# Moving work on TensorE in four attention stages of a transformer kernel, with repeated matmuls ahead of one of them

## What is computed

```python
x = x + _L1_xattn_ref(_layernorm(x), ctx, ctx, mask, ...)      # 16 heads, softmax over 77 keys
...
scores = jnp.einsum('bqhd,bkhd->bhqk', q, k) / np.sqrt(DK)     # _L1_ffn_ref: self attention,
attn = jax.nn.softmax(scores, axis=-1)                         # 16 heads of 16, 1024 x 1024 per head
o = jnp.einsum('bhqk,bkhd->bqhd', attn, v)
...
def sparse_norm(scores, nbias):                                # _L2_xattn_ref: no softmax
    t = jax.nn.relu(scores + nbias[0])
    t = t * t
    return t / (t.sum(-1, keepdims=True) + IEPS)
...
x = x + _L3_xattn_ref(_layernorm(x), ctx, ...)                 # 16 heads, softmax over 77 keys
```

## Time and profile before

| | |
|---|---|
| median of 3 runs | 2685.7 us (2677.44 to 2688.1) |
| the profiled execution | 2695.88 us |
| its span, first to last instruction | 2694.1 us |
| granted TensorE clock, mean | 0.887 |
| TensorE busy | 2201.1 us (82%) |
| VectorE busy | 1298.8 us (48%) |
| ScalarE busy | 1087.3 us (40%) |
| GpSimd busy | 651.7 us (24%) |

### The profile page before, as it was taken

The page is one execution under the profiler, slowest core; times in us unless marked ns, Lnnn a source line. Parts: engine busy times, 40 slices in busy tenths (PEclk is TensorE's granted clock), DMA queues, the critical chain, the costliest instruction groups (busy, mean ns, idle before and its releaser), DMA issues. The chain is left out here.

```text
span 2694.1 us, 36343 instructions
## 1 busy us (share of the span) xinstructions
PE 2201.1 (82%) x12198; PEld 1304.1 (48%) x12199; DVE 1298.8 (48%) x2560; ACT 1087.3 (40%) x2189; POOL 651.7 (24%) x569
## 2 busy tenths in 40 slices
PE   5899999953948766999998399994976999767786
PEld 2333333242933431333333299994345999633454
DVE  5655555165154557578871600004452350164785
ACT  3434444420314511566666244442532444325111
POOL 1238888911520050000000022220001222110011
PEclk9899999985977885699999699997887999978898
DMA  2000000022610053223420665652036666400000
GB/s 64 5 1 13 13 10 13 25 67 91 203 59 1 20 148 40 32 32 45 51 33 1 190 214 195 199 191 89 1 118 233 198 201 203 138 13 1 0 1 32
DMA packets 141630, 214.34 MB, mean 80 GB/s; under 512 B 39600, under 2 KB 97644, under 8 KB 141500
## 3 DMA queue, kind: packets, MB, share of 16 engines
q1 hardware_dynamic: 131228, 186.10, 25.3%
q0 software_dynamic: 9696, 26.49, 2.6%
q10 hardware_dynamic: 576, 0.07, 0.0%
HBM read 182.00 MB, written 30.15 MB: 79 GB/s over the span
## 5 line engine op out<-in xcount | busy, mean ns | idle before, releaser
L1840 DVE TENSOR_REDUCE heads_part_max<-heads_shared_ps 128x2 f32<-128x1024 f32 x256 | 300.1, 1220 | 93.5 <-PE heads_shared_ps L1757 93.5
L1824 ACT ACTIVATE heads_probs<-heads_score_ps 128x512 f32<-128x512 f32 x512 | 266.4, 603 | 194.4 <-PE heads_score_ps L1779 194.4
L2873 PE MATMUL experts_up_ps<-experts_rowT,experts_w 128*128 128x128 f32 x2864 | 342.9, 279 | 0.0
L2873 PEld LDWEIGHTS experts_up_ps<-experts_rowT,experts_w 128*128 128x128 f32 x2864 | 334.9, 195 | 0.2
L3033 DVE TENSOR_TENSOR experts_y<-experts_down_ps,experts_b_now 128x256 f32<-128x256 f32 x78 | 33.1, 425 | 499.5 <-PE experts_down_ps L2883 499.3
L1354 POOL TENSOR_TENSOR core_xT<-core_xT,heads_probs 128x1024 f32<-128x1024 f32 (+1 forms) x112 | 264.4, 2360 | 24.0 <-ACT heads_probs L1527 10.5
L2941 ACT ACTIVATE experts_hT<-experts_up_ps,experts_b_now 128x128 f32<-128x128 f32 x624 | 222.8, 367 | 49.0 <-PE experts_up_ps L2873 11.8
L1566 DVE TENSOR_REDUCE heads_part_max<-heads_shared_ps 128x1 f32<-128x512 f32 x256 | 164.5, 686 | 146.7 <-PE heads_shared_ps L1396 146.5
L1779 PE MATMUL heads_score_ps<-heads_q,heads_k 66*128 66x512 f32 x512 | 199.4, 478 | 29.2 <-ACT heads_probs L1824 24.9
L2822 POOL DMA_INDIRECT y_dram<-experts_y,experts_index x101 | 99.4, 984 | 456.3 <-DVE experts_y L3033 412.0
L1527 ACT ACTIVATE heads_probs<-heads_score_ps 128x1024 f32<-128x1024 f32 x128 | 131.0, 1023 | 177.8 <-PE heads_score_ps L1423 177.8
(11 more groups left out here) (557 smaller groups left out, 3242.7 us busy)
## 6 DMA issues: line engine op xcount, KB each, us to landing
experts_w<-in_L_ffn_W SPq DMA_DIRECT2D x39, 1024.0 KB, 5.2
experts_w<-in_L_ffn_w SPq DMA_DIRECT2D x39, 1024.0 KB, 5.0
experts_w<-in_L_ffn_W SPq DMA_DIRECT2D x23, 512.0 KB, 4.0
experts_w<-y_dram SPq DMA_DIRECT2D x20, 512.0 KB, 4.7
experts_b_now<-in_L_ffn_b SPq DMA_DIRECT2D x78, 128.0 KB, 2.9
heads_q<-l_queries SPq DMA_DIRECT2D x32, 256.0 KB, 11.9
heads_k<-l_keys SPq DMA_DIRECT2D x32, 256.0 KB, 13.6
l1f_w<-in_L_ffn_W SPq DMA_DIRECT2D x8, 1024.0 KB, 10.6
```

The source lines that it names most:

```text
L1824: act.activation(probs[:, t % SLOTS_OF_PROBS, r, :], score_ps[:, i % RING, :], ACT.Exp, scale=SC).then_inc(exp_done, 1)
L1840: dve.tensor_reduce(part_max[:, g % 2, 2 * pair:2 * pair + 2, s, x], two, AX.X, ALU.max).then_inc(shared_read, 1)
L2873: done = pe.matmul(up_ps[:, f % 4, 0:SLOT], w1_sb[:, u, c, f * P:(f + 1) * P], rowT[:, u % 2, c, :], start=(c == 0), stop=(c == DC - 1))
```

## The change

There are three edits on TensorE's lists, and no other engine's list changes.

1. In x1 and x3, the four matmuls of `queries(m + 2)` no longer stand together behind block m: one stands behind each of its second to fifth peak jobs.
2. In x2, `score` waits once for both halves of ScalarE's reading (`score_read` at 2t) and then issues all four row tiles.
3. In heads1, the fourth score of each step moves behind the two peaks. And 28 matmuls are added whose results nobody reads: 128 x 128 bf16 weights, 512 columns, all into `sums_ps`. 18 of them (`BEFORE`) stand between the first maxima's transposition and step 0, and five in each of steps 0 and 1: one behind each of three scores and two peaks. Step 1 waits for all 28 before its values are written to `sums_ps`.

```diff
-            def queries(m):
-                for g in range(DC):
-                    n = DC * m + g
+            def query(m, g, c):
+                n = DC * m + g
+                if c == 0:
                     if n < 2:
                         pe.wait_ge(k_copied, n + 1)
                     elif n < 4:
                         pe.wait_ge(v_copied, n - 1)
                     else:
                         pe.wait_ge(q_copied, n - 3)
+                done = pe.matmul(banks[:, n % 4, :], w["q"][:, c, g * P:(g + 1) * P],
+                                 core.xT[:, c, m * 512:(m + 1) * 512], start=(c == 0), stop=(c == DC - 1))
+                if c == DC - 1:
+                    done.then_inc(q_done, 1)
...
                     for job in range(8 * m, 8 * (m + 1)):
                         peak(job)
-                    if m + 2 < T // 512:
-                        queries(m + 2)
+                        x = job - 8 * m
+                        if m + 2 < T // 512 and 1 <= x <= DC * DC:
+                            query(m + 2, (x - 1) // DC, (x - 1) % DC)
...
+                elif t:
+
+                    pe.wait_ge(score_read, 2 * t)
                 for two in range(2):
-                    if t:
-                        pe.wait_ge(probs_done if soft else score_read, 2 * (t - 1) + two + 1)
+                    if t and soft:
+                        pe.wait_ge(probs_done, 2 * (t - 1) + two + 1)
...
+        BEFORE, EARLY = 18, 2
...
+            def keep_running(times):
+
+                for _ in range(times):
+                    pe.matmul(sums_ps[:], q_narrow[:, 0, 0:P], q_narrow[:, 0, 0:512], start=True,
+                              stop=True).then_inc(rested, 1)
+
             for item in work_at[-1]:
                 share(item)
+            keep_running(BEFORE)
             for t in range(STEPS):
                 items = work_at[t]
-                for r in range(QUAD):
+                early = t < EARLY
+                for r in range(QUAD - 1):
                     score(t, r)
+                    if early:
+                        keep_running(1)
                 for item in items[0:2]:
                     share(item)
+                    if early:
+                        keep_running(1)
+                score(t, QUAD - 1)
+                if t == 1:
+                    pe.wait_ge(rested, BEFORE + EARLY * (QUAD + 1))
                 if t:
                     value(t - 1)
```

More of the change, by code:

```diff
@@ L515, in queries @@
                         pe.wait_ge(q_copied, n - 3)
+                done = pe.matmul(banks[:, n % 4, :], w["q"][:, c, g * P:(g + 1) * P],
+                                 core.xT[:, c, m * 512:(m + 1) * 512], start=(c == 0), stop=(c == DC - 1))
+                if c == DC - 1:
+                    done.then_inc(q_done, 1)
+            def queries(m):
+                for g in range(DC):
                     for c in range(DC):
-                        done = pe.matmul(banks[:, n % 4, :], w["q"][:, c, g * P:(g + 1) * P],
-                                         core.xT[:, c, m * 512:(m + 1) * 512], start=(c == 0), stop=(c == DC - 1))
-                    done.then_inc(q_done, 1)
+                        query(m, g, c)
             def peak(job):
@@ L1710, in quad_attention @@
         sums_copied, rsum_done = st.sem("sums_copied"), st.sem("rsum_done")
+        rested = st.sem("rested")
         block = st.block()
         LOADS = 8
+        BEFORE, EARLY = 18, 2
         @block.sync
```

## The result

The changed kernel takes 2645.8 us in the median (4 runs, 2639.11 to 2647.91), the kernel before beside it 2686.9 us (4 runs, 2677.44 to 2689.62): a ratio of 0.985, with an interval of 0.982 to 0.988, or 41 us less. The profiled execution took 2647.91 us (span 2646.2) at a mean granted clock of 0.898; before it was 2695.88 us at 0.887.

What follows compares the result with a forecast made beforehand. TensorE's own row of work was taken to bound heads1's loop, at a low clock first. Terms -20.3 - 13.5 - 12.7 + 0 = -46.5 us give 2649.4 profiled, less 10.2 to the median: 2639 us, range 2624 to 2671.

Steps and rivals of the forecast that it cites:

- likeliest case: Whole kernel: the forecast as it stands, 2639 us, with the clock held in heads1 and x2 unchanged; chance 0.54.
- Clock, -20.3: heads1: added matmuls raise the clock before step 0 and it holds, -20.3 us, ends -24 and +8.
- Order, -13.5: heads1, steps 2 to 107: fourth score behind the peaks fills a hole, 0.16 us a step, -13.5 us.
- as do the steps with transpositions, which wait for VectorE: heads1: steps with transpositions wait for VectorE already, so they gain nothing from the new order.
- Queries, -12.7: x1 and x3, first two blocks: queries spread between peak jobs, -6.0 and -6.7 us, together -12.7 if the clock holds.
- I take held: x1 and x3: the full clock holds through both blocks, giving -12.7 us; the other end is +3.
- The thin stretch: x1 and x3: stretch between the queries, 2.6 us, called a close call for holding the clock.
- Four row tiles, 0: x2: waiting for all four row tiles moves nothing, 0 us, ends -1 and +1.
- VectorE taking the whole gain: Rival, heads1: both peaks wait for VectorE and steps stay at 2.93 us; 2652.5 us, chance 0.11.
- Queries that never see the full clock: Rival, x1 and x3: interleaved queries run at the low clock, +3 and not -12.7; 2655 us, chance 0.14.
- The clock that falls in step 0 or 1: Rival, heads1: the 18 matmuls raise the clock, it falls in steps 0 and 1; -16.5, 2669 us, chance 0.11.
- The slower case: Rival, heads1: clock falls in step 0 or 1, new order never raises it; up to 2835 us, chance 0.04.

Runs made afterwards that it cites:

- e2_keep: The kernel before with the 28 added matmuls alone, scores in their old order; median 2670.7 us, ratio 0.9969.
- e3_queries: The kernel before with only the queries of x1 and x3 spread between peak jobs; median 2680.4 us, ratio 0.9996.
- e4_x2: The kernel before with x2's single wait alone; median 2684.4 us, ratio 1.0015.
- f2_spread: The changed kernel with the query matmuls behind every second peak job (1, 3, 5, 7 of a block); median 2631.5 us, ratio 0.980 to before.
- g1_best: The changed kernel with queries behind jobs 1, 3, 5, 7 and without the ten added matmuls in steps 0 and 1; median 2631.5 us, ratio 0.983.
- g2_best_fill: The changed kernel with queries behind every second job, no added matmuls in steps 0 and 1, three f32 matmuls added in x2; median 2632.5 us.
- f3_half_reduce: The changed kernel with VectorE's maxima in heads1 taken over only 256 of each 512 columns; one run, 2619.6 us.
- e1_order: The kernel before with only the fourth score moved behind the peaks, no added matmuls; median 2680.4 us, ratio 0.9996.
- g4_six: The changed kernel with six added matmuls ahead of step 0 and none in steps 0 and 1; 2668.7 us, ratio 0.995.

## Why the prediction was right, and where it wasn't

The forecast was 2639 us (2624 to 2671); 2645.8 lies inside, 7 us above it. Its likeliest case came true in heads1 and x2. That the total is so close is in part luck. Against several profiles of each order, the clock gave 5 us and the queries 7 us less than forecast, and the order 4.5 us more. In the profiled pair the fall of 48.0 us meets the sum of 46.5 only because x2 and the five pieces without an edit, forecast at 0, fell by 4.3 us between them.

- **Clock, -20.3: right mechanism, some 5 us too large.** Step 0 began 2.35 us later against the stage's start (+2.2 forecast), steps 0 and 1 took 0.5 us less (0.6), the clock held. e2_keep's heads1 is 19.6 us shorter than that of the profiled execution before. But that execution had 15 low steps; e3_queries and e4_x2, with the same code there, had 12, and against their 568.9 us the term is -15. The prediction subtracted 10.2 us for the way from the profiled execution to the median and still took the full -20.3: if those two profiles are typical, part of the 10.2 us were low steps, and they were counted twice.
- **Order, -13.5: right mechanism, too small.** It measured -18.0. Forecast were plain steps of 2.64 and 2.89 us; they are 2.64 and 2.84, and the alternation starts anew with 2.64 behind each copy, so ten plain steps in sixteen gain 2.07 us. The unseen change from row tiles to the full array cost 0.11 us (0.33 from 1216.76 to 1217.09, less 0.213 of streaming) and not 0.15. The failed step is "as do the steps with transpositions, which wait for VectorE": the pairs of steps with one fell from 6.28 and 7.10 us in e2_keep to 5.98 and 6.67, 0.73 us in sixteen steps. 2.8 us in sixteen, times 106/16, is 18.5, near the 18.0 of the stage.
- **The rule on tiling modes** in the Trainium skill (TensorEngine Tiling, Key Properties) speaks of a drain at each change of mode. The trace agrees that a change costs, with 0.11 us for the one added here; it doesn't decide, because it is paid out of a hole of 0.54 us. At the low clock, where there was no hole to fill, it does decide: 4.71 us against 4.62.
- **Queries, -12.7: the failed step is "I take held".** Rounds of 1.30 and 1.43 us came as forecast in the first blocks, and ahead of the second blocks' queries the clock fell: in the changed kernel for all four queries in x1 and the first two in x3. Over seven profiles with this order x1 and x3 average 146.8 and 117.5 us, over the four without it 148.3 and 121.3: -5.3 us. The thin stretch, which the text took at 2.6 us and called a close call, measured 2.95 us in x3 and 3.50 in x1 and was the cause: f2_spread, g1_best and g2_best_fill, without it, average 140.2 and 113.5 us, which is -15.9.
- **Four row tiles, 0: right.** e4_x2 lies at 1.0015 (0.9996 to 1.0035), and scores to mask is 1.03 us. The 3.07-fold speedup that the Trainium skill (TensorE: Matmul & The Clock Gate, Part 3) measures for four tiles at once found nothing to speed up: the distance was 1.0 us with two tiles late or none. x2's -1.9 us is the clock's: its low stretch varies between profiles of the same code.
- **The rivals.** VectorE taking the whole gain fell with steps of 2.84 us, and f3_half_reduce shows the part that it does take, 0.20 us in every second step. Queries that never see the full clock came true for the second block of x1 and half of that of x3. The clock that falls in step 0 or 1 didn't come in the changed kernel, but g2_best_fill shows that it exists where the ten early matmuls are missing. The slower case didn't come, though its doubt was sound: in the three profiles that ran the new order at the low clock, it stayed low for 17 to 19 steps where the old order had 12 to 15, and then rose.
- **What the sum left out:** that order and clock multiply. The order's price is per step and depends on the clock of that step; the prediction priced it so (0.1 for a low step), but only as a rival. And in e1_order the low stretch itself was 7 steps longer than in e3_queries and e4_x2. Without the added matmuls the same edit is worth nothing measurable.

## What to carry to other kernels

Filling a hole in TensorE's loop pays only where TensorE isn't slow anyway: first get the clock up, then judge the order, and test both together, since in heads1 the matmuls alone gave 15 us, the order alone 4, and both 33. Where dense and thin work share an engine, spread the dense pieces evenly up to the end of the thin ones: with a tail of 3 us of thin work interleaving gave 5 us here, spread evenly 16. And take a term's size against several executions of the kernel before, not the one that was profiled, if its clock varies.

## What the runs showed of the hardware

- Work that holds the full clock can leave a low clock low for a long time. In e1_order TensorE counts as busy for 79.75 of 80 us and stays at 0.50, the 1.2 GHz level; the same loop at 1.00 is busy for some 215 of 220 us and stays there. 18 full-array bf16 matmuls in a row raised it in all nine profiles that have them; six did not, in the one profile that has six.
- Peaks alone for 2.95 us (x3) and 3.50 us (x1) of the changed kernel were followed by a fall of the clock, in both stages of all seven profiles with that order. With a query behind every second job it stayed at 1.00 through both blocks, in all three profiles.
- The rise comes at another place from run to run: 5 of the 18 passes ran slow in g2_best_fill, 10 in the changed kernel. The Trainium skill (TensorE: Matmul & The Clock Gate, Part 1) says that the number of slow matmuls at the start of a kernel varies from run to run, and the trace agrees for the start of a dense run inside the kernel. That an early rise can be followed by a fall, 36 us worse, was not expected.
- What ends a low stretch in a running loop stays open. In the old order it ended after 12, 12 and 15 steps. In the new one (e1_order, g2_best_fill, g4_six) it ended each time at the first transposition of the sums ahead of step 19, within its eight matmuls or up to 1.3 us behind them, at 1145, 1138 and 1144 us, though in g2_best_fill it had begun only in step 1. No experiment moved that transposition, and DMAs run there too; nor is it shown that the new order is what made the stretch longer.
- x2 runs through a low stretch in some profiles (129 to 134 us) and hardly or not at all in others (124 to 125) with the same code in it. That is up to 10 us, near the 0.5% that a measurement can tell.
